# Turning the normalized input in 32 by 32 blocks on VectorE and through DRAM, and the work behind it one batch later

## The reference

```
# layer 0
h   = relu(LN(x));  A^ = adj + I;  d = rowsum(A^)^-1/2
x   = x + relu((d A^ d h) W0^T + b0)
# layer 1
h   = relu(LN(x))                         # 256 nodes x 256 features: "the normalized input" of the change
c   = relu(bn1(conv1_w h^T))              # a product over the features
c   = bn2(conv2(c)), 17 taps along nodes; x_conv = relu(c + h^T)^T
s   = h w_se^T + b_se                     # 3 values a node
A   = exp(-|s_n - s_m|^2);  msg = relu(h w_msg^T + b_msg);  x_nmp = A msg
gates r, z, n of a GRU cell from [x_conv, x_nmp] and h
x   = x + (1 - z) n + z h
```

## Time and profile before

| | before |
|---|---|
| time, median of 3 runs | 1773.56 us (1773.48 to 1773.76) |
| the profiled execution | 1773.39 us, its span 1771.6 us |
| PE busy | 1757.3 us, 99% of the span |
| DVE, ACT, POOL busy | 68%, 56%, 46% of the span |
| first stage | about 0 to 657 us |
| TensorE clock granted, whole span | 0.999 |

### The profile page before, as it was taken

The page is one execution under the profiler, slowest core; times in us unless marked ns, Lnnn a source line. Parts: engine busy times, 40 slices in busy tenths (PEclk is TensorE's granted clock), DMA queues, the critical chain, the costliest instruction groups (busy, mean ns, idle before and its releaser), DMA issues.

```text
span 1771.6 us, 30896 instructions
## 1 busy us (share of the span) xinstructions
PE 1757.3 (99%) x10778; PEld 1556.6 (88%) x10778; DVE 1201.1 (68%) x2318; ACT 999.2 (56%) x1787; POOL 817.7 (46%) x988
## 2 busy tenths in 40 slices
PE   8999999999999999999999999999999999999998
PEld 7999999999999999999988888888888888888887
DVE  8999999999999956655664544544545545545445
ACT  6888888888888866666642333332333333333322
POOL 5788888888777637655731221221221212212211
PEclk9999999999999999999999999999999999999999
DMA  6567666666666454444674345445345353454442
GB/s 223 174 201 214 203 211 205 211 204 200 197 192 202 147 167 156 168 166 166 238 213 105 71 105 123 97 107 113 74 112 122 88 119 82 98 120 99 104 96 42
DMA packets 531865, 262.70 MB, mean 148 GB/s; under 512 B 366215, under 2 KB 494471, under 8 KB 531710
## 3 DMA queue, kind: packets, MB, share of 16 engines
q1 hardware_dynamic: 531166, 260.66, 53.5%
q10 hardware_dynamic: 544, 0.07, 0.0%
HBM read 151.58 MB, written 109.05 MB: 147 GB/s over the span
## 4 chain that ended last, share of the span: by engine, by line
PE 96%; issue 1%; DVE 1%; POOL 1%; DMA 1%; ACT 0%; SPq 0%; POOLq 0%; ACTq 0%; DVEq 0%
PE P L111 73%; PE P L618 6%; PE P L1025 4%; PE P L877 4%; PE P L647 4%; PE P L709 4%; PE P L666 2%; PE P L627 1%; DMA at<-in_adjt 0%; POOL axl L581 0%; DMA eye<-in_eye 0%; POOL af L578 0%; DVE sm L489 0%; DVE sm L495 0%; DVE xct L1039 0%
## 5 line engine op out<-in xcount | busy, mean ns | idle before, releaser
L1004 POOL TENSOR_TENSOR xnx1l<-xnf,xnx1h 128x1024 fp32r<-128x1024 f32 x16 | 44.3, 2771 | 393.2 <-ACT xnx1h L997 393.2
L1004 POOL TENSOR_TENSOR xnx0l<-xnf,xnx0h 128x1024 fp32r<-128x1024 f32 x15 | 40.9, 2729 | 272.9 <-ACT xnx0h L997 272.9
L1130 ACT ACTIVATE nn<-gn,col 128x512 f32<-128x512 f32 x64 | 46.4, 725 | 193.4 <-DVE gn L1151 193.4
L1127 ACT ACTIVATE tr<-P,cold 128x512 f32<-128x512 f32 x64 | 44.2, 690 | 179.8 <-PE P L111 179.8
L1147 DVE SCALAR_TENSOR_TENSOR gn<-tr,gn 128x512 f32<-128x512 f32 x64 | 45.2, 706 | 137.3 <-ACT tr L1127 137.3
L578 POOL TENSOR_TENSOR af<-af,at 128x512 f32<-128x512 f32 x64 | 111.9, 1748 | 40.8 <-ACT af L369 39.7
L581 POOL TENSOR_TENSOR axl<-af,axh 128x512 fp32r<-128x512 f32 x64 | 102.8, 1606 | 54.0 <-ACT axh L387 54.0
L618 PE MATMUL P<-ah,hd 128*128 128x256 f32 x512 | 121.9, 381 | 0.0
L1160 DVE SCALAR_TENSOR_TENSOR tz<-tz,tr 128x512 f32<-128x512 f32 x63 | 43.6, 692 | 109.3 <-ACT tz L1141 109.2
L1141 ACT ACTIVATE tz<-P,cold 128x512 f32<-128x512 f32 x63 | 43.4, 689 | 123.2 <-PE P L111 123.2
L111 PE MATMUL P<-w1mh,xxh 128*128 128x512 f32 x256 | 106.5, 416 | 0.0
(11 more groups left out here) (214 smaller groups left out, 6401.3 us busy)
## 6 DMA issues: line engine op xcount, KB each, us to landing
xh_d<-xst SPq DMA_DIRECT2D x64, 320.0 KB, 4.9
y_d<-yo SPq DMA_DIRECT2D x80, 256.0 KB, 2.1
yt<-y_d SPq DMA_DIRECT2D x128, 160.0 KB, 4.5
xl<-xh_d SPq DMA_DIRECT2D x36, 512.0 KB, 4.5
x<-in_x SPq DMA_DIRECT2D x64, 256.0 KB, 2.7
a<-in_adj SPq DMA_DIRECT2D x64, 256.0 KB, 3.0
at<-in_adjt SPq DMA_DIRECT2D x64, 256.0 KB, 4.2
x_d<-x SPq DMA_DIRECT2D x64, 256.0 KB, 4.4
```

Source lines behind the costliest of these rows:

```text
L1004: e.e.tensor_tensor(o[1][:, :, :], xnf[p % 2][:, :, :, :].rearrange("p c i t -> p c (i t)"), o[0][:, :, :], ALU.subtract).then_inc(done, 1)
```

## The change

The four transposes on PE, the copy `xt` on ACT and the store of `xt` go. In their place:

- ACT writes `xn` as (half of the features, half of the nodes, 128 features), and DVE transposes it in 32 by 32 blocks into `xnb`, one `STREAM_TRANSPOSE` of 128 by 512.
- SP stores `xnb` by four DMAs, one for each 32 partitions, so that the blocks come to lie in their transposed places in `xn_d[b]`. Each DMA moves 32 x 16 runs of 32 elements (128 bytes). A turn later one DMA loads `xn_d[b]` into `xt`, which now has two buffers, in 512 runs of 512 bytes.
- ACT makes `xxh` out of `xt` in SBUF and DVE makes `xxl` out of it, in turn b+6 and not b+5. Everything that follows from them (`s`, `cm`, `uv`, `dist`, `am`, `msl`, `nmp`, `dft`) is one turn later as well: there are 76 turns, 8 buffers `at`, and the filter units start one turn later.
- `uvh` moves from DVE to ACT. The steps of DVE and ACT stand in another order.
- `x`, `adj` and `adjt` come laid out by partition, so that each partition's load is one run of 2 KB and not two of 1 KB. `xn_d` is read in the third stage by pairs in runs of 512 bytes (before: 4 KB).
- A few start-up semaphores are merged.

```
@@ buffers and views
-    xn_d = nc.dram_tensor("xn_d", (NP, 128, 2, 2, 256), F32, kind="Internal").ap()
+    xn_d = nc.dram_tensor("xn_d", (NB, 4, 128, 128), F32, kind="Internal").ap()
-        xn = p1("xn", [128, 2, 256])
-        xt = p1("xt", [128, 512])
+        xn = p1("xn", [128, 2, 2, 128])
+        xt = [p1("xt0", [128, 512])]
...
+        xt.append(p1("xt1", [128, 512]))
+        xnb = p1("xnb", [128, 4, 4, 32])
-        TURNS = NB + 11
+        TURNS = NB + 12
@@ SP
+        def store_blocks(e, b):
+            e.wait_ge(S["xnb"], b + 1)
+            for a in range(4):
+                o = xn_d[b][:, :, 32 * a:32 * a + 32].rearrange("s (q j) i -> j (s q) i", j=32)
+                e.e.dma_start(o, xnb[32 * a:32 * a + 32, :, :, :].rearrange("j s q i -> j (s q) i")).then_inc(S["sxn"], 16)
+        def load_turned(e, b):
+            e.wait_ge(S["sxn"], 64 * (b + 1))
+            e.wait_ge(S["xxlo"], b - 1)
+            e.e.dma_start(xt[b % 2][:, :].rearrange("p (s n) -> p s n", s=4),
+                          xn_d[b].rearrange("s p n -> p s n")).then_inc(S[f"xt{b % 2}"], 16)
...
+            if live(i, 5):
+                load_turned(e, i - 5)
...
             if live(i, 4):
-                b = i - 4
-                e.wait_ge(S["x2"], b + 1)
...
-            if live(i, 5):
-                b = i - 5
-                e.wait_ge(S["xt"], b + 1)
-                e.e.dma_start(xn_d[b // 2][:, :, b % 2, :],
-                              xt[:, :].rearrange("p (c t) -> p c t", c=2)).then_inc(S["sxt"], 16)
+                store_blocks(e, i - 4)
@@ ACT
-                    t = e.e.activation(xn[:, n, :], x2[b % 2][:, n, :], ACT.Relu,
+                    t = e.e.activation(xn[:, :, n, :], x2[b % 2][:, n, :].rearrange("p (c k) -> p c k", c=2), ACT.Relu,
...
-                e.e.copy(xt[:, :], P[SXN][:, :]).then_inc(S["xt"], 1)
...
+                e.e.copy(uvh[0:96, :, :], uvf[0:96, :, :]).then_inc(S["uvh"], 1)
@@ DVE
-                e.e.tensor_tensor(xx[1][:, :], P[SXN][:, :], xx[0][:, :], ALU.subtract).then_inc(S["xxlo"], 1)
...
-                e.e.tensor_scalar(uvh[0:96, :, :], uvf[0:96, :, :], 1.0, None, ALU.mult).then_inc(S["uvh"], 1)
...
+                e.e.tensor_tensor(xx[1][:, :], xt[b % 2][:, :], xx[0][:, :], ALU.subtract).then_inc(S["xxlo"], 1)
...
+            if live(i, 4):
+                b = i - 4
+                e.wait_ge(S["xn"], b + 1)
+                e.wait_ge(S["sxn"], 64 * b)
+                e.e.transpose(xnb[:, :, :, :].rearrange("p s q i -> p (s q i)"),
+                              xn[:, :, :, :].rearrange("p c t k -> p (c t k)")).then_inc(S["xnb"], 1)
@@ PE
-            if live(i, 4):
-                b = i - 4
-                e.wait_ge(S["xn"], b + 1)
...
-                for c in range(2):
-                    for n in range(2):
-                        t = e.e.transpose(P[SXN][:, c * 256 + n * 128:c * 256 + n * 128 + 128],
-                                          xn[:, n, c * 128:c * 128 + 128], ident[:, :])
-                t.then_inc(S["xnt"], 1)
```

More of the change, by code:

```diff
@@ L115 @@
 NAMES = """
-half one ident_in col_in eye2_in w0_in b0_in tt_in w1_in se_in bm_in ft_in gt_in tap0 tap1 s2t
+ident_in col_in eye2_in w0_in b0_in tt_in w1_in se_in bm_in ft_in gt_in tap0 tap1 s2t
 consts crs diag rows normrow w1s chi clo ones taps
 ldx0 ldx1 lda0 lda1 lat0 lat1 st0 ag0a ag0 deg0 degm rs0 dd sd sbias hd ah agg aghi aglo
-out0 u x2 sx20 sx21 st1 ag1a ag1 rs1 n1b xn xnt xt sxt xxhi xxlo s uvf uvh uv cm0 cm1 tcm0 tcm1 h1 mshi mslo
+out0 u x2 sx20 sx21 st1 ag1a ag1 rs1 n1b xn xnb xt0 xt1 sxn xxhi xxlo s uvf uvh uv cm0 cm1 tcm0 tcm1 h1 mshi mslo
 dist af am axhi axlo nmp nm snm dft0 dft1 xe0 xe1 sxa0 sxa1 sxb0 sxb1
@@ L167, in gnn_kernel @@
         raw_wg = [third(f"st_wg{c}", [128, 768]) for c in range(6)]
-        xnf = [third(f"xnf{i}", [128, 2, 2, 256]) for i in range(2)]
+        xnf = [third(f"xnf{i}", [128, 2, 512]) for i in range(2)]
         nms = [third(f"nms{i}", [128, 2, 256]) for i in range(2)]
@@ L327, in spectrum_out, with message_hi @@
             e.e.copy(dst, src).then_inc(S[f"xe{c}"], 1)
+        def message_hi(e, b):
+            e.wait_ge(S["tcm0"], b + 1)
+            e.wait_ge(S["tcm1"], b + 1)
+            e.wait_ge(S["nmp"], b)
+            e.e.activation(ms[0][:, :, :], tcm[:, :, 256:512], ACT.Relu).then_inc(S["mshi"], 1)
         def relu(e, b):
@@ L341, in first_scalar @@
                 e.wait_ge(S["s"], b)
-                e.e.copy(xx[0][:, :], xt[:, :]).then_inc(S["xxhi"], 1)
-            if live(i, 6):
-                b = i - 6
-                e.wait_ge(S["tcm0"], b + 1)
-                e.wait_ge(S["tcm1"], b + 1)
-                e.wait_ge(S["nmp"], b)
-                e.e.activation(ms[0][:, :, :], tcm[:, :, 256:512], ACT.Relu).then_inc(S["mshi"], 1)
-            if i >= NB + 2 and live(i, 6):
-                relu(e, i - 6)
+                e.e.copy(xx[0][:, :], xt[b % 2][:, :]).then_inc(S["xxhi"], 1)
             if live(i, 4):
@@ L387, in first_scalar @@
                 e.e.copy(ax[0][:, :], af[:, :]).then_inc(S["axhi"], 1)
-            if live(i, 7):
-                spectrum_out(e, i - 7, 1)
-            if i < NB + 2 and live(i, 6):
-                relu(e, i - 6)
-            if live(i, 7):
-                b = i - 7
-                e.wait_ge(S["nmp"], b + 1)
-                e.wait_ge(S["snm"], 16 * b)
-                e.e.copy(nm[:, :], P[NMP][:, :]).then_inc(S["nm"], 1)
+            for c in range(2):
+                if live(i, 8):
+                    spectrum_out(e, i - 8, c)
+            if live(i, 6):
+                b = i - 6
+                e.wait_ge(S["uvf"], b + 1)
+                e.e.copy(uvh[0:96, :, :], uvf[0:96, :, :]).then_inc(S["uvh"], 1)
             if live(i, 1):
@@ L1480, in _ @@
             e = Engine(tensor)
-            e.wait_ge(S["one"], 1)
+            e.wait_ge(S["ones"], 2)
             for n in range(26):
```

243 lines of the change are left out of this document (118 added, 125 removed).

## The result

The changed kernel takes **1785.59 us** (median; 1784.46 to 1787.67), against 1773.52 us of the kernel before on the same chip: 1.007 of its time, with a 95% interval of 1.0052 to 1.0087. It is slower by 12.1 us where 25 us less were forecast. The profiled execution spans 1784.5 us, against 1771.6.

A forecast was written before the change was run, and what follows sets the result against it. PE's work and a ring through VectorE both bound the turn at 9.80 us. 64 x 0.48 = 30.7, less 2.7, 1.7, 1 and 0.4, leaves 24.9 off 1773.39: 1748.5 us (forecast 1743 to 1754; 1743 to 1774 holds 0.8).

The forecast's parts named there:

- the ring through VectorE: Waits through `agl`, `nmp`, `msh`, `xxh` and `xxl` on PE, ScalarE and VectorE: 19.60 us per two turns, 9.80 each.
- PE's term: Full turn on PE: four transposes (0.40 us) and 0.08 behind them go, so 9.80 becomes 9.32 us.
- The 0.08 behind the transposes: PE's first product after the transposes takes 0.20 us, the next 0.12; the extra was expected to go, else turn 9.40.
- VectorE's term: VectorE's work in a full turn: idle, `x2`'s wait and `uvh` go, block transpose comes; 8.80 us, 0.5 below PE.
- the collision with POOL: `x2` on VectorE starts inside POOL's `am` and takes 1.67 us, not 0.68; 0.99 us a turn of waiting.
- something takes the 0.99 back: No-change rival: the ring through `agl` stays at 9.8 us; 1777 us, or 1773 with half regained; chance 0.06.
- the rival that put the collision in the row `x2`, `xxl`, `msl`: POOL's tap and small operations collide with these VectorE steps; turns 10.3 us in 37 turns, 1785 us; chance 0.11.
- The margin of 0.3 us at `xxl`: `xxl` on VectorE ends at 4.4 us, usable 0.1 later; PE's `s` needs it at 4.8: tightest wait.
- New waits and the DMA work: Stores and load through DRAM priced at nothing, 1.5 us left at worst; DMA at most 8.9 of 9.3 us.
- The fill: Stage start, one more filling turn: 2.7 us new idle, 1.7 of transposes giving nothing, 0.4 of lower clock.
- The drain: Stage end: emptying takes one more round of waits of a few tenths, priced at 1 us.
- The prediction's rule: Port pair shared by VectorE and GpSimd is an exclusive lock, held a whole instruction by whoever starts first.

The follow-up runs named there:

- the order alone: The kernel before with one step of VectorE moved, `x2` directly behind `u`, transposes kept: 1774.49 us, 1.0004 of the kernel before.
- the degree first: The changed kernel with adj's row sums and the degree's mask and degree operations moved ahead of the statistics of x on VectorE: 1765.56 us, 0.9957 of before.
- the three edits: The changed kernel with degree's operations ahead of x's statistics, `tt_w` load earlier, `xxh` and `xxl` earlier in the last turns: 1757.09 us, 0.9907 of before.

## Why the prediction was wrong, point by point

- **What bounds the kernel now: right.** TensorE's own work and the ring through VectorE were equal. Either relief alone changed the mean turn by 0.03 and 0.06 us, both together by 0.44.
- **PE's term: right in kind, 0.04 to 0.07 us too large.** Forecast were 0.48 us and a turn of 9.32; measured are a turn of 9.36 and a price of 0.41 (9.77 - 9.36) to 0.44 us (9.80 - 9.36). The 0.08 behind the transposes did go. But the 0.40 of the earlier trace rows held some waiting: in the kernel with the order alone, in which VectorE is early, it is 0.36 (407.40 to 407.76). Over 64 turns 0.04 to 0.07 is 2.6 to 4.5 us.
- **VectorE's term: this is the step that failed.** "Sum: 9.80 - 0.18 - 0.99 + 0.62 - 0.45 = 8.80 us [...] If the collision with POOL only moved to another step it would be 9.79. I take 8.80". It was 9.78. `x2`'s 0.99 were gained, the block transpose cost its 0.70 and `uvh` went; then `axl` took 0.86 back at the mask. The paragraph on where the steps fall placed `axl` "beside row sums and `tcm1`", which is where it is, and asked of the steps beside it only whether they read two tensors in SBUF. It passed over the two operations between row sums and `tcm1`, of 0.15 us each. The bound was in the text, 9.79, and by the prediction's own rule the time for it was 1777 ("something takes the 0.99 back"), at a chance of 0.06 for that case; the rival that put the collision in the row `x2`, `xxl`, `msl` had 1785 us, close to what came, but for another place and by another mechanism: those three ran at 0.69 us each. A smaller miss is in the same sum: 9.78 - 0.86 = 8.92 is 0.12 above 8.80, and in the kernel with the degree first VectorE has 0.21 us of idle time a turn ahead of `tcm0`, not up to 0.5.
- **The margin of 0.3 us at `xxl`: right and harmless.** PE's wait of 0.21 ahead of `s` goes when VectorE isn't late.
- **ScalarE: right. POOL: right in its list, wrong in its length.** The same list took GpSimd 438.6 us over the 53 turns and 410.8 before, 0.53 us a turn more, though `am` got shorter: its small operations beside VectorE's two-input steps got longer (below). So the rival's mechanism was there in part. It isn't enough for the turn by itself: behind the taps GpSimd has 0.35 us to spare ahead of `am` and the turn is still 9.67. With the three edits the list took 410.7 again. How much of the turn GpSimd's longer list costs while the taps run, no run separates from the mask's wait.
- **New waits and the DMA work: right.** With a turn of 9.36 and TensorE never idle, the four stores, the load and their packets cost nothing in the full turns. The stores land 2.4 us after issue (2.2 in the changed kernel) and the share of DMA time is 0.92, where the prediction had at most 8.9 of 9.3.
- **The fill: mis-sized.** The new idle time was put at 2.7 us, with 1.7 for transposes that give nothing and 0.4 of clock. It was 9.8. 2.5 of it (17.14 less 14.62) are the table's load: the prediction went through SyncE's queue for the full turns and not for the constants that SyncE loads once, between the turns. The other 7.3 are work that isn't there, since the `u` come when they came before: by the estimate above 4.7 us of one batch's products, put off by the extra turn, where the prediction had the gap in one filling turn, 5.7 less 3.0, and 3.1 us of transposes that give nothing, those of seven batches, where it had three or four turns and 1.7. Over fill and drain together the 0.48 didn't come either: TensorE's busy time in both rose by 0.4 us (71.39 + 72.98 against 79.04 + 64.93), with a granted clock of 0.92 in the fill, where it had been 0.98. How much of it the clock took wasn't measured.
- **The drain: mis-sized.** "Emptying takes one more round of waits of a few tenths, 1 us." It was 6.0, and 4.5 of it (7.54 less 3.06) an order: ScalarE's `xxh`, first of the turn before the change, had been put behind `msh` and `h`, which costs nothing in a full turn and a wait for this turn's products in an empty one.
- **The sum.** Forecast -24.9; in the profiled executions +12.9. Of the 37.8 between them 22.2 are the full turns (25.4 less 3.2), 10.0 the ends of the stage (15.8 of idle time, less the 5.8 priced), and 5.7 the transposes of the other 11 turns, 5.3, which TensorE's busy time there should have lost, while it rose by 0.4.
- **No change elsewhere: right.** The stages behind took 1099.11 us against 1099.18.

## What to carry to other kernels

Where VectorE or GpSimd works all the time, go through every step of one beside every step of the other, also those that take 0.15 us: a tiny single-source operation on two columns in SBUF waited 0.86 us for GpSimd, and written a column at a time it didn't. When a pipeline is made a turn deeper, read the empty turns and the one-time loads as closely as the full turn: an order that is free when all engines are busy cost 4.5 us in the drain, and a load that fell behind a store's wait 2.5 us in the fill. Where two engines are the bound by turns, relief of one alone is worth next to nothing: here 0.03 and 0.06 us a turn, against 0.44 for both. And price an extra turn of filling by the work that it puts off, here some 4.7 us by the estimate, not by the gap in one filling turn, here 2.7.

## What the hardware showed that I had not expected

- A 128x2 `TENSOR_SCALAR` in SBUF, 0.15 us alone, lasts until GpSimd's running 128x512 operation ends (1.02 us); four on one column each, inside the same operation, take 0.33 together. Batch statistics, their aggregates and row sums beside GpSimd's two-input operations kept their times. So did the block transpose, 0.70 to 0.71 us in all 64; in 37 of them it ran beside GpSimd's work on the taps, and beside a two-input operation in the third stage.
- It goes the other way too. GpSimd's small operations beside VectorE's row of two-input steps are held; this one takes 0.34 us with the degree first, where it falls elsewhere. The changed kernel, lowest, median and highest ns:

```profile
L568 POOL TENSOR_TENSOR sm<-sm x64: 194/615/622, 6.9 to 605.5; 128x2 f32<-128x2 f32 x64
```

- The two collisions aren't alike. Where `x2`, with two inputs, fell into `am`, both were long, 1.67 and 1.82 us. Where the mask fell into `axl`, the mask alone was (1.02, and `axl` 1.29, as without it). The prediction's rule, the whole instruction held by whoever starts first, fits the second and not the first; why, no run here tells.
